# Five PSUM banks in a ring for the wide product between the two passes of layer 3

## The chip, the cores and the metric

The kernel runs on one NeuronCore of a Trainium2 chip. The metric is the device time of one execution in microseconds, lower is better. Everything happens in one launch: four layers of a graph network, each with an attention or mixing branch and a mixture-of-experts block.

## The reference, cut to what matters

There are 3125 nodes with 256 features, held as 25 tiles of 125 rows. Layer 3's graph branch is two steps of a heterogeneous graph transformer. Between the two edge passes each node row goes through this:

```python
# end of step 0, h: [3125, 256] summed messages; x: [3125, 256]
h = segment_sum(m * att[:, :, None], dst).reshape(n, 256)
h = h @ Wa[0]
x = h * sigmoid(skip[0]) + x * (1.0 - sigmoid(skip[0]))
# start of step 1: keys and values per edge type, and the query
k, q, v = x @ Wk[1], x @ Wq[1], x @ Wv[1]
kw = einsum(k[src], Watt[1][:, etype]);  m = einsum(v[src], Wmsg[1][:, etype])
```

The kernel folds `Watt` and `Wmsg` into the key and value weights beforehand. What is left for each tile is one product with a 256x256 matrix (`Wa`, the sigmoid folded in), an add, and one wide product with a 256x1280 matrix: 1024 columns go to a table in HBM from which the edges gather, and 256 are the query, which stays in SBUF. All of it is fp32.

## The kernel before, in words

The stage is one call of `renew` (name `l3_hgt0_out`, in the trace `l_hgt_out`, where digits are left out of names). `hgt` makes it with `part` (the node sums of the edge pass) and with `onward` (the wide product), and it is the only call that has both. Its engines run without a scheduler. Each has a loop over rounds `i` written out in order, and semaphores tie them. In round `i`:

- TensorE turns tile `i` of the node sums (line 1927, into `pt0`), multiplies tile `i-1` by the 256x256 matrix (line 1935, into `out0`: the first product), turns tile `i-4` of the new rows (line 1943, into `pt1`), and makes the wide product of tile `i-5` (line 1963, into `out1`). The wide product has three column groups, of 512, 512 and 256 columns, each in its own PSUM bank and with two matmuls in the code, for the two halves of the contraction. Each fp32 matmul of the code shows as two MATMULs in the trace, so a wide product is x12 there.
- VectorE divides tile `i` of the sums (line 2073), adds the first product of tile `i-1` into `x` (line 2078), and then empties two groups of the wide product of tile `i-6`: group 0, 512 columns, into `rows` (line 2118), and group 2, the query (line 2120). A drain and the signal `s_take` follow (line 2127).
- ScalarE copies the turned tiles to SBUF (lines 1976 and 1993) and empties group 1 into `rows` (line 1999, signal `s_half`).
- SyncE waits for `s_take` and `s_half` and stores the 1024 columns of the tile to the table (lines 1898 and 1899). `rows` has four slots.

PSUM has eight banks, and this stage has all of them: one for `pt0`, two for `out0`, two for `pt1`, and three for `out1`. The wide product has a single set of three banks (`B1 = 1`), so the product of tile `t` waits until both VectorE and ScalarE have emptied all of tile `t-1`:

```python
if t >= B1:
    pe.wait_ge(s_take, t - B1 + 1)
    if passing > 512 or twin:
        pe.wait_ge(s_half, t - B1 + 1)
```

Of the kernel before, what the change touches and what calls it, by code (L numbers as in the profile page):

```python
# [14 lines left out]
P = 125  # L15
# [1788 lines left out]
def renew(core, name, x, xn, mix=None, part=None, fetch=None, norm=True, onward=None, keep=None, out=None, square=None, beside=None):  # L1804
# [10 lines left out]
    passing = onward.get("passing", 0) if wide else 0  # L1815
    of, s_of = xn if norm else x, None
    mixed = part["acc"] if part else xn
    B0, B1 = (1, 1) if part and wide else (2, 2)
    last_on_vector = onward.get("last") if wide else None
    gain = fetch.get("gain") if fetch else None  # L1820
    finite = fetch.get("finite") if fetch else False
# [2 lines left out]
    with Phase(core, name) as ph:  # L1824
# [91 lines left out]
        if mix or wide:  # L1916
            @block.tensor
            def _(pe):
                for i in range(NT + 5):
                    t = i  # L1920
                    if mix and t < NT:
                        if t >= B0:
                            pe.wait_ge(s_xt0, t - B0 + 1)
                        if part:
                            pe.wait_ge(s_even, t + 1)
                        for k in range(2):
                            mm = pe.transpose(pt0[:, t % B0, P * k:P * k + P], mixed[:, t, 128 * k:128 * k + 128], core.ident[0:P, 0:P])
                        mm.then_inc(s_turn0, 1)
                    t = i - 1
                    if mix and 0 <= t < NT:  # L1930
                        pe.wait_ge(s_xt0, t + 1)
                        if t >= 2:
                            pe.wait_ge(s_x, t - 1)
                        for k in range(2):
                            mm = pe.matmul(out0[:, t % 2, 0:D], xt0[:, t % 2, k, :], a[:, k, :], start=k == 0, stop=k == 1)
                        mm.then_inc(s_mm0, 1)
                    t = i - 4
                    if wide and 0 <= t < NT:
                        pe.wait_ge(s_of, t + 1)
                        if t >= 2:  # L1940
                            pe.wait_ge(s_xt, t - 1)
                        for k in range(2):
                            mm = pe.transpose(pt1[:, t % 2, P * k:P * k + P], of[:, t, 128 * k:128 * k + 128], core.ident[0:P, 0:P])
                        mm.then_inc(s_turn, 1)
                        if square is not None:
                            for k in range(2):
                                pe.matmul(p_square[:, k, 0:D], of[:, t, 128 * k:128 * k + 128], of[:, t, :],
                                          start=t == 0, stop=t == NT - 1, skip_group_check=True)
                                mm = pe.matmul(p_square[:, k, D:D + 1], of[:, t, 128 * k:128 * k + 128], core.ones[0:P, 0:1],
                                               start=False, stop=t == NT - 1, skip_group_check=True)  # L1950
                            mm.then_inc(s_square, 1)
                    t = i - 5
                    if wide and t >= 0:
                        if t == 0 and loads:
                            pe.wait_ge(s_load, 16 * len(loads))
                        pe.wait_ge(s_xt, t + 1)
                        if t >= B1:
                            pe.wait_ge(s_take, t - B1 + 1)
                            if passing > 512 or twin:
                                pe.wait_ge(s_half, t - B1 + 1)  # L1960
                        for n, (c, d) in enumerate(cuts):
                            for k in range(2):
                                mm = pe.matmul(out1[:, t % B1, n, 0:d - c], xt_of(t)[:, k, :], w[:, k, c:d], start=k == 0, stop=k == 1)
                        mm.then_inc(s_mm, 1)

        @block.scalar
        def _(act):
            if norm:
                act.wait_ge(s_eps, 1)
            for i in range(NT + 6):  # L1970
                t = i
                if mix and t < NT:
                    act.wait_ge(s_turn0, t + 1)
                    if t >= 2:
                        act.wait_ge(s_mm0, t - 1)
                    act.copy(xt0[:, t % 2, :, :].rearrange("p k c -> p (k c)"), pt0[:, t % B0, 0:2 * P]).then_inc(s_xt0, 1)
                if gain is not None and t < NT:
                    act.wait_ge(s_var0, t + 1)
                    act.activation(sd[:, 0, t:t + 1], mv[:, 0, t, 1:2], ACT.Sqrt, bias=eps[:, 0:1]).then_inc(s_sd0, 1)
                t = i - 2  # L1980
                if norm and 0 <= t < NT:
                    act.wait_ge(s_var, t + 1)
                    act.activation(sd[:, 1, t:t + 1], mv[:, 1, t, 1:2], ACT.Sqrt, bias=eps[:, 0:1]).then_inc(s_sd, 1)
                t = i - 3
                if norm and 0 <= t < NT:
                    act.wait_ge(s_shift, t + 1)
                    act.activation(xn[:, t, :], x[:, t, :], ACT.Identity, bias=mv[:, 1, t, 0:1], scale=sd[:, 1, t:t + 1]).then_inc(s_xn, 1)
                t = i - 4
                if wide and 0 <= t < NT:
                    act.wait_ge(s_turn, t + 1)  # L1990
                    if t >= 2 and kept_xt is None:
                        act.wait_ge(s_mm, t - 1)
                    act.copy(xt_of(t).rearrange("p k c -> p (k c)"), pt1[:, t % 2, 0:2 * P]).then_inc(s_xt, 1)
                t = i - 6
                if passing > 512 and t >= 0:
                    act.wait_ge(s_mm, t + 1)
                    if t >= 4:
                        act.wait_ge(s_store[t % 4], 32 * (t // 4))
                    act.copy(rows[:, t % 4, 512:passing], out1[:, t % B1, 1, 0:passing - 512]).then_inc(s_half, 1)
                if twin and t >= 0:  # L2000
                    act.wait_ge(s_mm, t + 1)
                    act.copy(dst[:, t, 0:M - passing], out1[:, t % B1, 1, 0:M - passing]).then_inc(s_half, 1)

        @block.vector
        def _(v):
# [61 lines left out]
            for i in range(NT + 6):  # L2067
# [7 lines left out]
                if 0 <= t < NT:  # L2075
                    if part:
                        v.wait_ge(s_mm0, t + 1)
                        o = v.scalar_tensor_tensor(out=x[:, t, :], in0=part["old"][:, t, :], scalar=part["rest"], in1=out0[:, t % 2, 0:D], op0=ALU.mult, op1=ALU.add)
                        if back is not None:
                            v.wait_ge(s_back[t % 4], 32 * (t // 4 + 1))  # L2080
                            v.drain()
                            o = v.tensor_tensor(x[:, t, :], x[:, t, :], back[:, t % 4, :], ALU.add)
                        o.then_inc(s_x, 1)
                        v.drain()
                    elif mix:
                        if cvec is not None:
                            v.tensor_tensor(x[:, t, :], x[:, t, :], cvec[:, :], ALU.add)
                        v.wait_ge(s_mm0, t + 1)
                        v.drain()
                        v.tensor_tensor(x[:, t, :], x[:, t, :], out0[:, t % 2, 0:D], ALU.add).then_inc(s_x, 1)  # L2090
                        v.drain()
                    if fetch and gain is None:
                        fetched(t)
# [12 lines left out]
                                           op0=ALU.mult, op1=ALU.mult).then_inc(s_shift, 1)  # L2106
                t = i - 6
                if wide and t >= 0:
                    v.wait_ge(s_mm, t + 1)
                    if t == 0 and loads:  # L2110
                        v.wait_ge(s_load, 16 * len(loads))
                    if passing:
                        if t >= 4:
                            v.wait_ge(s_store[t % 4], 32 * (t // 4))
                        if twin:
                            v.tensor_tensor(rows[:, t % 4, :], out1[:, t % B1, 0, 0:passing], bias[:, 0:passing], ALU.add)
                        else:
                            v.tensor_copy(rows[:, t % 4, 0:min(passing, 512)], out1[:, t % B1, 0, 0:min(passing, 512)])
                    if passing and not twin:
# [1202 lines left out]
```

## Time and profile before

| | us |
|---|---|
| median of 3 runs | 7434.0 (7430.2 to 7436.23) |
| the profiled execution: its own time | 7426.5 |
| its span, first to last instruction | 7424.3 |
| this stage: first instruction of `l_hgt_out` to the last signal of its product | 5788.07 to 5992.09 |
| POOL's one wait that covers the stage and the end of the pass before | 314.4 |

The profile is one execution. Its page gives each engine's busy share of the whole span: PE (TensorE matmul) 69%, DVE (VectorE) 64%, POOL (GpSimd) 47%, ACT (ScalarE) 38%. These are averages over some forty stages with different limits, and the stage between the passes is under 3% of the span. So it has to be read from its own stretch of the timeline. In a timeline row the first number is the start in us from the start of the span, the second how long the merged instructions took, then the engine, the line of the kernel, the operation, output and inputs by name, the shape, and how many instructions were merged. In brackets stands the idle time of that engine just before, and what ended it. The end of a matmul is modelled, so the distance from one start to the next is the surer number. PEld is the load of the stationary operand, which runs beside the matmuls.

### The profile page before, as it was taken

To read this page: it belongs to the slowest core of one execution; us is meant where nothing else is said; L and a number is where in the kernel's file an instruction comes from. 1 tells how busy PE (TensorE), PEld (TensorE's weight loads), DVE (VectorE), ACT (ScalarE), POOL (GpSimd) and SP (SyncE) were. 2 spreads that over 40 slices of the span, in tenths; PEclk is the share of its full clock that TensorE was granted. 3 is DMA by queue.
4 is the path that set the end of the run, shared out by engine and by line. 5 is a ranking of instruction groups with operands and counts; after the bars stand their busy time and mean duration, and the time that the engine had idled before them with its cause. 6 is when DMAs were issued, how large, how long until landed. Compare 5 with 4: busy or idle time off the path is not lost. (4 is left out here: it accounts for less than half of the span.)

```text
span 7424.3 us, 107945 instructions
## 1 busy us (share of the span) xinstructions
PE 5125.7 (69%) x21553; PEld 3617.6 (49%) x21554; DVE 4752.9 (64%) x11861; ACT 2828.9 (38%) x6921; POOL 3525.0 (47%) x3532
## 2 busy tenths in 40 slices
PE   4763677767774967768666676877776767776764
PEld 4763444444443834558543356744444444444453
DVE  6875477677776158551556663279997369996453
ACT  2551255345534220012223222237775147772331
POOL 1776277537740257741167702236664046661014
PEclk9999877687776988979867778999998999997887
DMA  3442244324431943338334416857674156662036
GB/s 88 163 146 64 77 128 127 87 80 127 129 68 64 321 130 102 104 82 314 128 94 108 104 33 208 273 158 212 210 211 137 45 173 210 206 209 53 19 119 195
DMA packets 523813, 1021.65 MB, mean 138 GB/s; under 512 B 143645, under 2 KB 284498, under 8 KB 514846
## 3 DMA queue, kind: packets, MB, share of 16 engines
q0 software_dynamic: 191360, 489.21, 24.5%
q1 hardware_dynamic: 301663, 497.07, 20.8%
q10 hardware_dynamic: 30528, 32.52, 1.3%
q8 instruction: 87, 1.43, 0.1%
q14 instruction: 175, 1.43, 0.1%
HBM read 927.97 MB, written 90.27 MB: 137 GB/s over the span
## 5 line engine op out<-in xcount | busy, mean ns | idle before, releaser
L733 POOL DMA_INDIRECT l_hgt_ep_g<-l_tkm,l_hgt_ep_ix x832 | 922.4, 1109 | 442.8 <-PE l_hgt_ep_out L831 239.2
L744 POOL DMA_INDIRECT l_gat_ep_g<-l_gat_th,keep_e_src x832 | 865.1, 1040 | 433.8 <-issue 230.7
L831 PE MATMUL l_gat_ep_out<-l_gat_ep_g,l_gat_ep_here 128*126 128x264 f32 x1664 | 716.8, 576 | 136.6 <-DVE l_gat_acc L988 133.2
L831 PEld LDWEIGHTS l_gat_ep_out<-l_gat_ep_g,l_gat_ep_here 128*126 128x126 f32 x1664 | 394.4, 268 | 366.4 <-DVE l_gat_acc L988 297.5
L2472 DVE TENSOR_TENSOR f_moe_experts_yb<-f_moe_experts_py,f_moe_experts_b2s 128x256 f32<-128x256 f32 x208 | 88.3, 425 | 711.9 <-PE f_moe_experts_py L2455 687.5
L831 PE MATMUL l_hgt_ep_out<-l_hgt_ep_g,l_hgt_ep_here 128*126 128x288 f32 x1664 | 501.0, 425 | 55.6 <-DVE l_hgt_ep_g L974 54.0
L2423 POOL DMA_INDIRECT f_moe_experts_xg<-f_moe_tx,f_moe_tok x208 | 197.2, 948 | 699.7 <-PE f_moe_experts_px L2436 613.8
L872 ACT COPY l_gat_ep_stage<-l_gat_ep_out 30x264 f32<-30x264 f32 x832 | 307.4, 371 | 540.8 <-PE l_gat_ep_out L831 532.1
L2487 ACT ACTIVATE f_moe_experts_ht<-f_moe_experts_phid,f_moe_experts_b1b 128x128 f32<-128x128 f32 x848 | 241.3, 372 | 667.2 <-PE f_moe_experts_phid L2446 663.7
L525 POOL DMA_INDIRECT recs<-place_stage,place_pos x392 | 424.8, 1084 | 138.5 <-issue 116.8
L2744 POOL DMA_INDIRECT l_edges_g<-l_table,keep_e_src x416 | 410.3, 986 | 147.0 <-issue 120.7
L2446 PE MATMUL f_moe_experts_phid<-f_moe_experts_xt,f_moe_experts_w1b 128*128 128x128 f32 x3392 | 429.4, 281 | 68.9 <-DMA f_moe_experts_b1b<-in_L_ffn_b 60.7
L744 POOL DMA_INDIRECT l_ep_g<-l_table,keep_e_src x416 | 407.3, 979 | 126.6 <-issue 122.1
L805 PE MATMUL l_hgt_ep_found<-l_q,l_hgt_ep_hot 125*128 x1664 | 431.2, 404 | 25.5 <-ACT l_hgt_ep_hot L848 20.6
L2446 PEld LDWEIGHTS f_moe_experts_phid<-f_moe_experts_xt,f_moe_experts_w1b 128*128 128x128 f32 x3392 | 402.7, 195 | 90.6 <-issue 65.6
L831 PE MATMUL l_ep_out<-l_ep_g,l_ep_here 128*126 128x257 f32 x832 | 334.5, 556 | 106.7 <-DVE l_acc L988 100.8
L2455 PE MATMUL f_moe_experts_py<-f_moe_experts_w2b,f_moe_experts_ht 128*128 128x256 f32 x1696 | 401.4, 381 | 0.0
L872 ACT COPY l_hgt_ep_stage<-l_hgt_ep_out 126x288 f32<-126x288 f32 x832 | 307.6, 394 | 222.1 <-PE l_hgt_ep_out L831 210.0
L988 DVE TENSOR_TENSOR l_gat_acc<-l_gat_acc,l_gat_ep_out 125x264 f32 x832 | 344.3, 414 | 68.3 <-issue 48.2
L988 DVE TENSOR_TENSOR l_hgt_acc<-l_hgt_acc,l_hgt_ep_stage 125x288 f32 x832 | 370.3, 445 | 24.1 <-ACT l_hgt_ep_stage L872 14.8
L831 PEld LDWEIGHTS l_hgt_ep_out<-l_hgt_ep_g,l_hgt_ep_here 128*126 128x126 f32 x1664 | 285.7, 191 | 181.8 <-issue 133.8
L805 PEld LDWEIGHTS l_hgt_ep_found<-l_q,l_hgt_ep_hot 125*128 125x128 f32 x1664 | 310.5, 197 | 99.2 <-issue 62.0
(638 smaller groups left out, 11723.2 us busy)
## 6 DMA issues: line engine op xcount, KB each, us to landing
l_hgt_ep_hot<-locrow SPq DMA_DIRECT2D x208, 256.0 KB, 4.9
f_moe_experts_w1b<-in_L_ffn_w SPq DMA_DIRECT2D x32, 1024.0 KB, 6.5
f_moe_experts_w2b<-in_L_ffn_w SPq DMA_DIRECT2D x32, 1024.0 KB, 7.3
f_moe_experts_w1b<-in_L_ffn_w SPq DMA_DIRECT2D x64, 512.0 KB, 5.0
f_moe_experts_w2b<-in_L_ffn_w SPq DMA_DIRECT2D x64, 512.0 KB, 5.2
f_moe_experts_w1b<-in_L_ffn_W SPq DMA_DIRECT2D x56, 512.0 KB, 5.0
f_moe_experts_w2b<-in_L_ffn_W SPq DMA_DIRECT2D x56, 512.0 KB, 5.4
l_gat_ep_hot<-locrow SPq DMA_DIRECT2D x104, 256.0 KB
```

Source lines behind the costliest of these rows:

```text
L525: gp.indirect_dma_start(recs, bass.IndirectOffsetOnAxis(ap=pos[:, b, j:j + 1].bitcast(U32), axis=0), stage[:, b, j, :], None).then_inc(sca ...
L733: gp.indirect_dma_start(g[:, b % NB, j, 0:W], None, table, bass.IndirectOffsetOnAxis(ap=ix[:, b, j:j + 1].bitcast(U32), axis=0)).then_inc( ...
L744: gp.indirect_dma_start(g[:, k % NB, j, 0:W], None, table, bass.IndirectOffsetOnAxis(ap=idx[:, k * CT + j:k * CT + j + 1].bitcast(U32), ax ...
L805: mm = pe.matmul(found[:, h, j * D:j * D + D], hot[0:P, b % 2, 128 * (h * HT + j):128 * (h * HT + j) + 128], look[:, bass.ds(blks[h * HT + ...
L831: pe.matmul(out[:, t % 4, 0:WO], here[:, b % 2, t, :], g[:, b, t, F:F + WO], start=True, stop=True).then_inc(s_out, 1)
L872: act.copy(stage[lo:P + 1, b % 2, t, :], out[lo:P + 1, t % 4, 0:WO]).then_inc(s_staged, 1)
L988: v.tensor_tensor(slot, slot, stage[0:P, b % 2, t, :] if kind == "hgt" else out[0:P, t % 4, 0:WO], ALU.add).then_inc(s_added, 1)
L2423: gp.indirect_dma_start(xg[:, b, :], None, tx, bass.IndirectOffsetOnAxis(ap=tok[:, t:t + 1].bitcast(U32), axis=0)).then_inc(s_x[b], 16)
L2446: mm = pe.matmul(phid[:, b % 2, 128 * f:128 * f + 128], w1b[:, b, k, 128 * f:128 * f + 128], xt[:, b % 2, k, :], start=(k == 0), stop=(k = ...
L2455: mm = pe.matmul(py[:, b % 2, 0:D], ht[:, b % 2, f, :], w2b[:, b, f, :], start=(f == 0), stop=(f == FC - 1))
L2487: act.activation(ht[:, b % 2, f, :], phid[:, b % 2, 128 * f:128 * f + 128], func, bias=b1b[:, b, f:f + 1])
L2744: gp.indirect_dma_start(g[:, i % RB, j, :], None, table, bass.IndirectOffsetOnAxis(ap=core.e_src[:, i * EG + j:i * EG + j + 1].bitcast(U32 ...
```

## The change

Only the call with both `part` and `onward` changes (`shared` is true there). `out0` and `pt1` go from two banks to one each, and the two banks go to `out1`, which then has five. The column groups of all tiles are counted through, `3 * t + n`, and group number `g` goes to bank `g % 5`. Before TensorE writes a group it waits for the engine that empties the group five earlier, and for nothing else. For this the emptying of group 0 gets its own signal (`s_first`), next to `s_half` for group 1 and `s_take` for group 2. Group 0 and group 1 each get a signal of their own when they are made (`s_cut[0]`, `s_cut[1]`), and VectorE and ScalarE wait for these. VectorE waits for `s_mm` only before it copies group 2.

```diff
-    B0, B1 = (1, 1) if part and wide else (2, 2)
+    shared = part is not None and wide
+    B0, B1 = 1 if shared else 2, 2
...
-            out0 = ph.psum("out0", [P, 2, 512])
+            out0 = ph.psum("out0", [P, B0, 512])
...
-            pt1 = ph.psum("pt1", [128, 2, 512])
-            out1 = ph.psum("out1", [P, B1, len(cuts), 512])
+            pt1 = ph.psum("pt1", [128, B0, 512])
+            out1 = ph.psum("out1", [P, 1, 5, 512] if shared else [P, B1, len(cuts), 512])
+            s_cut = [ph.sem(f"cut{n}") for n in range(2)] if shared else []
+            s_first = ph.sem("first") if shared else None
+
+            def made_in(t, n, c):
+                return out1[:, 0, (len(cuts) * t + n) % 5, 0:c] if shared else out1[:, t % B1, n, 0:c]
...
                         pe.wait_ge(s_xt0, t + 1)
-                        if t >= 2:
-                            pe.wait_ge(s_x, t - 1)
+                        if t >= B0:
+                            pe.wait_ge(s_x, t - B0 + 1)
...
                         pe.wait_ge(s_of, t + 1)
-                        if t >= 2:
-                            pe.wait_ge(s_xt, t - 1)
+                        if t >= B0:
+                            pe.wait_ge(s_xt, t - B0 + 1)
...
                         pe.wait_ge(s_xt, t + 1)
-                        if t >= B1:
+                        if t >= B1 and not shared:
                             pe.wait_ge(s_take, t - B1 + 1)
...
                         for n, (c, d) in enumerate(cuts):
+                            if shared and len(cuts) * t + n >= 5:
+                                before, cut = divmod(len(cuts) * t + n - 5, len(cuts))
+                                pe.wait_ge((s_first, s_half, s_take)[cut], before + 1)
                             for k in range(2):
-                                mm = pe.matmul(out1[:, t % B1, n, 0:d - c], xt_of(t)[:, k, :], w[:, k, c:d], start=k == 0, stop=k == 1)
+                                mm = pe.matmul(made_in(t, n, d - c), xt_of(t)[:, k, :], w[:, k, c:d], start=k == 0, stop=k == 1)
+                            if shared and n < 2:
+                                mm.then_inc(s_cut[n], 1)
                         mm.then_inc(s_mm, 1)
...
-                    act.wait_ge(s_mm, t + 1)
+                    act.wait_ge(s_cut[1] if shared else s_mm, t + 1)
...
-                    v.wait_ge(s_mm, t + 1)
+                    v.wait_ge(s_cut[0] if shared else s_mm, t + 1)
...
+                    if shared:
+                        o.then_inc(s_first, 1)
+                        v.wait_ge(s_mm, t + 1)
+                        o = v.tensor_copy(dst[:, t, :], made_in(t, 2, M - passing))
```

No instruction changes its place on any engine. What moves are the waits. On TensorE in a round in the middle of the stage (first product, second turned tile, wide product), the order before was as follows. Semaphores are printed under the name of an earlier semaphore that had the same number: `l0_folds_cols` is `s_x`, `l0_in_store2` is `s_xt0`, `l0_in_sd` is `s_xt`, `l0_in_mm` and `l0_in_turn` are `s_half` and `s_take`.

```order
L1935 MATMUL l_hgt_out_out<-l_wa,l_hgt_out_xt 125x256 [waits l0_folds_cols,l0_in_store2]
L1935 MATMUL l_hgt_out_out<-l_wa,l_hgt_out_xt 125x256
L1943 MATMUL l_hgt_out_pt<-keep_ident,keep_x 128x125 [waits l0_in_sd,l0_folds_cols]
L1943 MATMUL l_hgt_out_pt<-keep_ident,keep_x 128x125
L1963 MATMUL l_hgt_out_out<-l_w,l_hgt_out_xt 125x512 [waits l0_in_mm,l0_in_turn,l0_in_sd]
L1963 MATMUL l_hgt_out_out<-l_w,l_hgt_out_xt 125x512 x3
L1963 MATMUL l_hgt_out_out<-l_w,l_hgt_out_xt 125x256 x2
```

In the changed kernel the same place reads as below, where `l0_mix_ms` is the new `s_first`.

```order
L1941 MATMUL l_hgt_out_out<-l_wa,l_hgt_out_xt 125x256 [waits l0_folds_cols,l0_in_store2]
L1941 MATMUL l_hgt_out_out<-l_wa,l_hgt_out_xt 125x256
L1949 MATMUL l_hgt_out_pt<-keep_ident,keep_x 128x125 [waits l0_in_sd,l0_folds_cols]
L1949 MATMUL l_hgt_out_pt<-keep_ident,keep_x 128x125
L1972 MATMUL l_hgt_out_out<-l_w,l_hgt_out_xt 125x512 [waits l0_in_mm,l0_in_sd]
L1972 MATMUL l_hgt_out_out<-l_w,l_hgt_out_xt 125x512
L1972 MATMUL l_hgt_out_out<-l_w,l_hgt_out_xt 125x512 [waits l0_in_turn]
L1972 MATMUL l_hgt_out_out<-l_w,l_hgt_out_xt 125x512
L1972 MATMUL l_hgt_out_out<-l_w,l_hgt_out_xt 125x256 [waits l0_mix_ms]
L1972 MATMUL l_hgt_out_out<-l_w,l_hgt_out_xt 125x256
```

The one wait ahead of the whole wide product for both emptying engines has become one wait ahead of each column group, each for one engine.

On VectorE a round of the same stretch was this before, where `l0_in_store3` is `s_mm0` (the first product is made), `l0_in_xn` is `s_mm` (the whole wide product is made), and `l0_in_square` is the store that last used the slot of `rows`.

```order
L2073 TENSOR_TENSOR l_hgt_acc<-l_hgt_acc,l_hgt_best 125x256
L2078 SCALAR_TENSOR_TENSOR keep_x<-keep_xn,l_alpha,l_hgt_out_out 125x256 [waits l0_in_store3]
L2118 COPY l_hgt_out_rows<-l_hgt_out_out 125x512 [waits l0_in_square,l0_in_xn]
L2120 COPY l_q<-l_hgt_out_out 125x256
L2073 TENSOR_TENSOR l_hgt_acc<-l_hgt_acc,l_hgt_best 125x256
```

It is now this, with `l0_mix_ts` for `s_cut[0]`.

```order
L2084 TENSOR_TENSOR l_hgt_acc<-l_hgt_acc,l_hgt_best 125x256
L2089 SCALAR_TENSOR_TENSOR keep_x<-keep_xn,l_alpha,l_hgt_out_out 125x256 [waits l0_in_store3]
L2129 COPY l_hgt_out_rows<-l_hgt_out_out 125x512 [waits l0_in_square,l0_mix_ts]
L2133 COPY l_q<-l_hgt_out_out 125x256 [waits l0_in_xn]
L2084 TENSOR_TENSOR l_hgt_acc<-l_hgt_acc,l_hgt_best 125x256
```

The wait for the whole product has gone from the first of the two copies to the second.

## Rows read from the trace of the kernel before

**Rows 1.** Waits from 5812 to 5996 us: in total, times, longest.

```profile
PE l_hgt_out_out L1963 <- DVEq L2127: 33.6, 21, 2.0
```

**Rows 2.** Timeline of one round in the middle: start us, us, engine, line.

```profile
5870.78 0.38 PE L1927 MATMUL l_hgt_out_pt<-keep_ident,l_hgt_acc 125*128 125x125 f32 x2
...
5871.00 1.03 PE L1935 MATMUL l_hgt_out_out<-l_wa,l_hgt_out_xt 128*125 128x256 f32 x4
...
5871.87 0.38 PE L1943 MATMUL l_hgt_out_pt<-keep_ident,keep_x 125*128 125x125 f32 x2
5872.07 0.48 DVE L2078 SCALAR_TENSOR_TENSOR keep_x<-keep_xn,l_alpha,l_hgt_out_out 125x256 f32<-125x256 f32 x1 [5.24 <-PE l_hgt_out_out L1935]
5872.28 0.37 ACT L1993 COPY l_hgt_out_xt<-l_hgt_out_pt 128x250 f32<-128x250 f32 x1 [0.71 <-PE l_hgt_out_pt L1943]
5872.55 0.59 ACT L1999 COPY l_hgt_out_rows<-l_hgt_out_out 125x512 f32<-125x512 f32 x1
5872.71 0.69 DVE L2118 COPY l_hgt_out_rows<-l_hgt_out_out 125x512 f32<-125x512 f32 x1 [0.16 <-issue]
5873.32 0.41 DVE L2120 COPY l_q<-l_hgt_out_out 125x256 f32<-125x256 f32 x1
...
5873.85 0.43 DVE L2073 TENSOR_TENSOR l_hgt_acc<-l_hgt_acc,l_hgt_best 125x256 f32<-125x256 f32 x1
5873.86 4.53 PE L1963 MATMUL l_hgt_out_out<-l_w,l_hgt_out_xt 128*125 128x512 f32 x12 [1.62 <-DVEq L2127]
...
5874.37 0.19 PEld L1963 LDWEIGHTS l_hgt_out_out<-l_w,l_hgt_out_xt 128*125 128x125 f32 x1 [0.24 <-issue]
...
5877.37 0.62 PEld L1963 LDWEIGHTS l_hgt_out_out<-l_w,l_hgt_out_xt 128*125 128x125 f32 x3 [0.24 <-issue]
...
5878.23 0.38 PE L1927 MATMUL l_hgt_out_pt<-keep_ident,l_hgt_acc 125*128 125x125 f32 x2
...
5878.45 1.03 PE L1935 MATMUL l_hgt_out_out<-l_wa,l_hgt_out_xt 128*125 128x256 f32 x4
...
5879.31 0.38 PE L1943 MATMUL l_hgt_out_pt<-keep_ident,keep_x 125*128 125x125 f32 x2
```

**Rows 3.** Timeline at the first two wide products.

```profile
5812.52 0.63 PE L1943 MATMUL l_hgt_out_pt<-keep_ident,keep_x 125*128 125x125 f32 x2
...
5812.94 6.17 PE L1963 MATMUL l_hgt_out_out<-l_w,l_hgt_out_xt 128*125 128x512 f32 x12
...
5818.94 0.38 PE L1927 MATMUL l_hgt_out_pt<-keep_ident,l_hgt_acc 125*128 125x125 f32 x2
...
5821.94 3.24 PE L1963 MATMUL l_hgt_out_out<-l_w,l_hgt_out_xt 128*125 128x512 f32 x7 [1.55 <-DVEq L2127]
```

**Rows 4.** Timeline of the last rounds, where no first product is left.

```profile
5980.72 4.53 PE L1963 MATMUL l_hgt_out_out<-l_w,l_hgt_out_xt 128*125 128x512 f32 x12 [1.04 <-ACT l_hgt_out_rows L1999]
...
5986.44 4.53 PE L1963 MATMUL l_hgt_out_out<-l_w,l_hgt_out_xt 128*125 128x512 f32 x12 [1.19 <-DVEq L2127]
...
5991.02 0.69 DVE L2118 COPY l_hgt_out_rows<-l_hgt_out_out 125x512 f32<-125x512 f32 x1 [4.70 <-PE l_hgt_out_out L1963]
5991.62 0.41 DVE L2120 COPY l_q<-l_hgt_out_out 125x256 f32<-125x256 f32 x1
5992.09 0.31 SPq L1898 DMA_DIRECT2D l_tkm<-l_hgt_out_rows  x1
```

**Rows 5.** Stretches: from:to, us, busy by engine, PE clock, DMA share, GB/s.

```profile
5760.00:5787.00 27.00, 26.44 (x97) 16.94 (x95) 19.61 (x49) 0.00 (x0) 0.00 (x0) 1.00 0.00 1
...
5870.00:5900.00 30.00, 23.16 (x81) 13.43 (x80) 7.72 (x16) 4.89 (x12) 0.00 (x0) 1.00 0.22 69
...
5963.00:5996.00 33.00, 23.31 (x66) 11.71 (x66) 5.35 (x11) 3.74 (x8) 0.31 (x2) 0.97 0.30 94
```

**Rows 6.** Timeline of the layer's earlier wide product, with two sets of banks.

```profile
4887.65 4.53 PE L1963 MATMUL f_out_out<-l_brief_w,f_out_xt 128*125 128x512 f32 x12 [0.87 <-issue]
...
4890.60 0.58 ACT L1999 COPY f_out_rows<-f_out_out 125x512 f32<-125x512 f32 x1
```

**Rows 7.** Waits of SyncE's queue from 5812 to 5996 us.

```profile
SPq L95 <- DMA l_tkm<-l_hgt_out_rows: 2.2, 1, 2.2
```

More of the change, by code:

```diff
@@ L1931, in _ @@
                         pe.wait_ge(s_xt0, t + 1)
-                        if t >= 2:
-                            pe.wait_ge(s_x, t - 1)
+                        if t >= B0:
+                            pe.wait_ge(s_x, t - B0 + 1)
                         for k in range(2):
-                            mm = pe.matmul(out0[:, t % 2, 0:D], xt0[:, t % 2, k, :], a[:, k, :], start=k == 0, stop=k == 1)
+                            mm = pe.matmul(out0[:, t % B0, 0:D], xt0[:, t % 2, k, :], a[:, k, :], start=k == 0, stop=k == 1)
                         mm.then_inc(s_mm0, 1)
@@ L1939, in _ @@
                         pe.wait_ge(s_of, t + 1)
-                        if t >= 2:
-                            pe.wait_ge(s_xt, t - 1)
+                        if t >= B0:
+                            pe.wait_ge(s_xt, t - B0 + 1)
                         for k in range(2):
-                            mm = pe.transpose(pt1[:, t % 2, P * k:P * k + P], of[:, t, 128 * k:128 * k + 128], core.ident[0:P, 0:P])
+                            mm = pe.transpose(pt1[:, t % B0, P * k:P * k + P], of[:, t, 128 * k:128 * k + 128], core.ident[0:P, 0:P])
                         mm.then_inc(s_turn, 1)
@@ L1992, in _ @@
                         act.wait_ge(s_mm, t - 1)
-                    act.copy(xt_of(t).rearrange("p k c -> p (k c)"), pt1[:, t % 2, 0:2 * P]).then_inc(s_xt, 1)
+                    act.copy(xt_of(t).rearrange("p k c -> p (k c)"), pt1[:, t % B0, 0:2 * P]).then_inc(s_xt, 1)
                 t = i - 6
                 if passing > 512 and t >= 0:
-                    act.wait_ge(s_mm, t + 1)
+                    act.wait_ge(s_cut[1] if shared else s_mm, t + 1)
                     if t >= 4:
                         act.wait_ge(s_store[t % 4], 32 * (t // 4))
-                    act.copy(rows[:, t % 4, 512:passing], out1[:, t % B1, 1, 0:passing - 512]).then_inc(s_half, 1)
+                    act.copy(rows[:, t % 4, 512:passing], made_in(t, 1, passing - 512)).then_inc(s_half, 1)
                 if twin and t >= 0:
@@ L2077, in _ @@
                         v.wait_ge(s_mm0, t + 1)
-                        o = v.scalar_tensor_tensor(out=x[:, t, :], in0=part["old"][:, t, :], scalar=part["rest"], in1=out0[:, t % 2, 0:D], op0=ALU.mult, op1=ALU.add)
+                        o = v.scalar_tensor_tensor(out=x[:, t, :], in0=part["old"][:, t, :], scalar=part["rest"], in1=out0[:, t % B0, 0:D], op0=ALU.mult, op1=ALU.add)
                         if back is not None:
@@ L2089, in _ @@
                         v.drain()
-                        v.tensor_tensor(x[:, t, :], x[:, t, :], out0[:, t % 2, 0:D], ALU.add).then_inc(s_x, 1)
+                        v.tensor_tensor(x[:, t, :], x[:, t, :], out0[:, t % B0, 0:D], ALU.add).then_inc(s_x, 1)
                         v.drain()
@@ L2117, in _ @@
                         else:
-                            v.tensor_copy(rows[:, t % 4, 0:min(passing, 512)], out1[:, t % B1, 0, 0:min(passing, 512)])
-                    if passing and not twin:
+                            o = v.tensor_copy(rows[:, t % 4, 0:min(passing, 512)], made_in(t, 0, min(passing, 512)))
+                    if shared:
+                        o.then_inc(s_first, 1)
+                        v.wait_ge(s_mm, t + 1)
+                        o = v.tensor_copy(dst[:, t, :], made_in(t, 2, M - passing))
+                    elif passing and not twin:
                         o = v.tensor_copy(dst[:, t, :], out1[:, t % B1, passing // 512, passing % 512:passing % 512 + M - passing])
```

## The prediction, made before the run

> **What bounds the kernel now.** I read the waits of the stage first, then its timeline, because the page's shares say nothing about a stage that is under 3% of the span. The list of waits has one long entry for TensorE: 21 of the 25 wide products wait for VectorE's signal behind its drain, 33.6 us in all [rows 1]. The reader is to see in one round of the timeline [rows 2] how that comes about. TensorE turns a tile at 5870.78, makes the first product at 5871.00, turns the second tile at 5871.87, and is then through at about 5872.1. But VectorE starts its add only at 5872.07, when the first product is complete. It copies group 0 at 5872.71 and the query at 5873.32, which ends at 5873.73, and only at 5873.86 does the next wide product start. The old product had been complete since before 5871. VectorE reaches it late because the add stands ahead of the copies in its order. So the stage is a loop of two engines: TensorE works 5.7 us, waits, and VectorE's chain of 2 us is exposed once per tile. The next round starts its turned tile at 5878.23, which is 7.45 us later. Nothing else is running that could hide this: DMA is busy 0.22 of the time and the clock is at its full level, 1.00 (2.4 GHz, the second row of [rows 5]). The stage ends in a barrier of all engines behind the last store [rows 7], so what it saves should come off the whole.
>
> **What a round takes without the wait.** From starts in [rows 2]: turned tile to first product 0.22 (5878.23 to 5878.45), first product to second turned tile 0.86 (to 5879.31). The second turned tile takes as long as the first, 0.22; early in the stage, where every step still took twice as long, it was 0.42 to the wide product behind it, with no wait between them (5812.52 to 5812.94) [rows 3], which fits. The wide product: weight loads at 5874.37 and 5877.37 with seven steps between them give 0.43 a step. Eight steps of 512 columns are 3.44, four of 256 columns at half that are 0.86, together 4.30. The measured 4.37 (5873.86 to 5878.23) has 0.07 more, because the first matmul behind a wait has a step of 0.50. The round is 0.22 + 0.86 + 0.22 + 4.30 = 5.60 us, against 7.45.
>
> **Do the new waits let it?** I count from the start of the second turned tile (call it 0); the wide product then starts at 0.22. Group 0 of tile t waits for ScalarE's group 1 of tile t-2, emptied a round ago. Group 1 waits for the query copy of t-2, also a round old. Group 2 waits for group 0 of t-1. VectorE adds at 0.20, copies group 0 from 0.84 to 1.53, and TensorE wants that bank at 0.22 + 3.44 = 3.66. That leaves 2.1 us. The turn of the next round needs VectorE's division (5873.85, ended 5874.28, so 2.41 on this count) at 4.52: another 2.1 us to spare. VectorE has 0.48 + 0.69 + 0.41 + 0.43 = 2.0 us of work in the round and ScalarE 0.37 + 0.37 + 0.59 = 1.3, so TensorE is the bound by far.
>
> **The banks given up.** With one bank for the first product, the product of tile t has to wait for the add of t-1. VectorE does this add before it divides tile t+1, and TensorE has already waited for that division in order to turn tile t+1. So the new wait is always met: cost nothing, and it can't cost anything. With one bank for the second turned tile, the next turn waits for ScalarE's copy, which ends 0.78 after the turn started (5871.87 to 5872.65) [rows 2], while the next turn comes 5.6 us later, or 4.5 in the last rounds. Nothing either.
>
> **The extra waits and signals.** Each wide product has three waits for banks, two of them in its middle, where before there was none. No row shows a met wait inside a wide product. The nearest rows are the joints between the turned tiles and the first product, which carry waits too and follow each other in 0.22 and 0.86 us, exactly what the matmuls take: 0. From the other side, a wait that really stops TensorE costs, beyond its length, 0.13 from the end of the query copy to the start (5873.73 to 5873.86) and the 0.07 of the slow first step, 0.20; three in each of 24 products would be 14.4 us. Below nothing is excluded, since a wait takes no matmul away. I take 0, because the joints are the same case: waits that are met before TensorE gets there. The wait added on VectorE and the two signals lie inside its 3.6 us of idle time per round.
>
> **The copies beside matmuls.** VectorE and ScalarE now read PSUM while TensorE writes other banks. In the earlier stage of the same form ScalarE's copy took 0.58 in the middle of a wide product [rows 6], against 0.59 here beside an idle TensorE [rows 2]. Cost 0.
>
> **The sum.** Tiles t = 0 to 24, from the start of wide product 0. To the next turned tile 6.00 (5812.94 to 5818.94, its first steps still twice as long) [rows 3], as before; then 1.30 to wide product 1. From 1 to 19, 18 rounds of 5.60 = 100.8. From 19 to 20 no tile of the sums is left to turn: 4.30 + 0.86 + 0.22 = 5.38. From 20 to 23 only the second turn is left: 3 x 4.52 = 13.56. From 23 to 24: 4.30. Together 131.3. Before, it was 5986.44 - 5812.94 = 173.5 [rows 3, 4]. Saved: 42.2. At the end the 512-column copy no longer waits for the whole product, so the query copy follows it at once: 5991.62 - 5991.02 = 0.6 [rows 4]. In all 42.8 us. A check from the other side: 33.6 us of waits [rows 1], and about 1.04 each for the three that ended on ScalarE (one is the first row of [rows 4]), are 36.7; the rows start an idle time at the modelled end of a matmul, some 0.16 late, and each restart costs 0.07, so 24 x 0.23 = 5.5 more: 42.2.
>
> The profiled execution took 7426.5, of which 7424.3 is its span; its sum is 7426.5 - 42.8 = 7383.7. The median of the runs is 7.5 above the profiled one, and I carry the saving over to it: 7434.0 - 42.8 = 7391.2.
>
> **Stores.** A tile's 500 KB now leaves every 5.6 us, and every 4.5 in the last rounds, 111 GB/s. At one tile per 5.75 us the queues moved 94 GB/s at a share of 0.30 (the third row of [rows 5]), so 0.36 is asked for. The last store landed within 2.2 us of its issue [rows 7], and four slots give 18 us. Nothing.
>
> **Rivals.**
>
> A, the waits inside the product show (8%): between the bounds above, up to 14.4 us of the gain is lost. At two thirds, 9.6, the time is 7401. Against it stand the joints in [rows 2].
>
> B, a new wait takes the place of the old one (4%): TensorE stands before group 2 until VectorE has emptied group 0. It decides once VectorE is 2.1 us later than in my count, for instance if its copies slowed beside matmuls. If only the query copy and its drain were hidden (0.5 a round, 24 times), the gain would be 12 us: 7422. Against it: ScalarE's copy in [rows 6].
>
> C, no effect (3%): the ring still waits for the same signal, or the next pass starts earlier and gives it back in its gathers: 7434. Against it: group 1's wait is for a tile older, as the changed order shows, and the barrier lies between.
>
> D, slower (3%): TensorE's clock falls in the stage. At 1.2 GHz a round would be 11.2 us, 3.75 more than now. For 18 rounds that is 67 us, and 9.0 against 5.75 in the last five another 16: some 7517. It decides from the point at which a third of a round is at the half clock (5.60 x 1.33 = 7.45). Against it: with TensorE busy 26.44 of 27.00 us the clock was 1.00, and at 23.16 of 30.00, with an idle gap in each round, also 1.00 [rows 5]; the ring makes those gaps smaller.
> The Trainium skill has a rule for this (TensorE: Matmul & The Clock Gate, "A second HAM failure mode: psum-queue depth-cycling"): a kernel that cycled through PSUM banks each iteration left small idle gaps between groups of matmuls, and its clock swung between the two levels. By that rule rival D would hold, by the two rows of 1.00 it doesn't; the trace so far disagrees with it.
>
> **How the numbers follow.** My forecast, all waits gone, has 82%: 7391. Its own range comes from the differences between runs (the profiled one 7.5 below the median, the three 6 apart) and from half of the bound on waits. For 8 in 10 I take 7382 to 7404; the upper end holds nearly all of rival A. Faster than 0.2% means below 7419; 0.2% is about what a measurement of this kernel can tell from no change. Forecast and A are faster, B is about half on either side: faster 0.93, same 0.04, slower 0.03.
>
> **What would show it.** In the new profile the distance between wide products in the middle is 5.6 us, with no idle time of PE before or inside a wide product; the row "PE waits for DVEq" of this stage is gone or under 1 us; VectorE's add follows each first product as before, and its wait there shrinks from 5.24 to about 3.4; the group 0 copy of the last tile starts before the product is complete; the whole stage is some 43 us shorter, and all stages behind it take as long as before. I am wrong if PE idles in steps of 0.2 inside a product (A), if it waits before group 2 (B), or if the clock is under 1.00 between the first and last wide product (D).

## The result

The changed kernel took 7391.1 us in the median of 5 runs (7383.2 to 7398.6), the kernel before, measured again beside it, 7430.2 (7417.4 to 7436.2). The ratio is 0.9949 with a 95% interval of 0.9937 to 0.9960: 38 us, or 30 to 47. A second set of runs on another chip gave 0.9937 (0.9920 to 0.9953). The prediction was 7391.2 and a gain of 42.8 us.

The span of the new profiled execution is 7383.8 us, 40.5 less. The first view is again one round in the middle of the stage, now of the changed kernel, with the columns of [rows 2].

```profile
5870.24 0.38 PE L1933 MATMUL l_hgt_out_pt<-keep_ident,l_hgt_acc 125*128 125x125 f32 x2
...
5870.46 1.03 PE L1941 MATMUL l_hgt_out_out<-l_wa,l_hgt_out_xt 128*125 128x256 f32 x4
...
5871.32 0.38 PE L1949 MATMUL l_hgt_out_pt<-keep_ident,keep_x 125*128 125x125 f32 x2
...
5871.53 0.48 DVE L2089 SCALAR_TENSOR_TENSOR keep_x<-keep_xn,l_alpha,l_hgt_out_out 125x256 f32<-125x256 f32 x1 [3.39 <-PE l_hgt_out_out L1941]
5871.54 4.46 PE L1972 MATMUL l_hgt_out_out<-l_w,l_hgt_out_xt 128*125 128x512 f32 x12
...
5872.17 0.69 DVE L2129 COPY l_hgt_out_rows<-l_hgt_out_out 125x512 f32<-125x512 f32 x1 [0.16 <-issue]
...
5872.77 0.41 DVE L2133 COPY l_q<-l_hgt_out_out 125x256 f32<-125x256 f32 x1
...
5873.31 0.43 DVE L2084 TENSOR_TENSOR l_hgt_acc<-l_hgt_acc,l_hgt_best 125x256 f32<-125x256 f32 x1
...
5875.84 0.38 PE L1933 MATMUL l_hgt_out_pt<-keep_ident,l_hgt_acc 125*128 125x125 f32 x2
```

The wide product starts 0.22 after the second turn with no bracket of idle time, where it had waited 1.62 us in [rows 2]. VectorE does the same things at the same distance from the first product as before, but nobody waits for them. From turn to turn it is 5.60 us (5870.24 to 5875.84) against 7.45.

The next rows are the last tile, and the stretch from product 1 to near the end of product 24, in the order of engines of [rows 5].

```profile
5940.82 8.76 PE L1972 MATMUL l_hgt_out_out<-l_w,l_hgt_out_xt 128*125 128x512 f32 x24
...
5947.04 0.69 DVE L2129 COPY l_hgt_out_rows<-l_hgt_out_out 125x512 f32<-125x512 f32 x1 [1.29 <-PE l_hgt_out_out L1972]
...
5949.62 0.42 DVE L2133 COPY l_q<-l_hgt_out_out 125x256 f32<-125x256 f32 x1 [1.89 <-PE l_hgt_out_out L1972]
5950.10 0.31 SPq L1904 DMA_DIRECT2D l_tkm<-l_hgt_out_rows  x1
```

```profile
5821.00:5949.00 128.00, 128.00 (x446) 74.90 (x445) 42.88 (x87) 27.22 (x66) 0.00 (x0) 1.00 0.31 97
```

TensorE is busy for all 128 us. From 5812 us on, where the list of [rows 1] began, it has one wait left, in the head and for VectorE's division. The second row is POOL's one wait that covers the stage, 314.4 us before:

```profile
PE l_hgt_out_pt L1933 <- DVE l_hgt_acc L2084: 0.8, 1, 0.8
POOL l_hgt_ep_ix L725 <- POOLq L95: 269.6, 1, 269.6
```

The row of 33.6 us [rows 1] is gone. The waits ahead of 5812 us, five for the division and 12.8 us in all, are in both kernels. I measure the stage from its first VectorE instruction (line 2006 before, 2017 after) to the issue of the last tile's first store. Before, that was 5788.07 to 5992.09, 204.0 us. Now it is 5789.64 to 5950.10, 160.5 us.

### The profile page after: what moved, and what is told of

It reads as the page before. It is cut to its first block and busy times, and to the rows that moved or that the text cites. A ratio compares the mean times of both kernels' runs of the same rounds, so it can differ in the third digit from the quotient of the medians.

```text
span 7383.8 us, 107946 instructions
## 1 busy us (share of the span) xinstructions
PE 5110.4 (69%) x21553; PEld 3608.4 (49%) x21554; DVE 4756.1 (64%) x11861; ACT 2831.3 (38%) x6921; POOL 3529.4 (48%) x3532
## 5 line engine op out<-in xcount | busy, mean ns | idle before, releaser
L805 PE MATMUL l_hgt_ep_found<-l_q,l_hgt_ep_hot 125*128 x1664 | 432.9, 405 | 26.7 <-ACT l_hgt_ep_hot L848 21.7
```

The source lines that it names most:

```text
L805: mm = pe.matmul(found[:, h, j * D:j * D + D], hot[0:P, b % 2, 128 * (h * HT + j):128 * (h * HT + j) + 128], look[:, bass.ds(blks[h * HT + ...
```

## The experiments

All stage lengths below are taken from the traces in that way. Rounds are the distances between the starts of successive wide products. A median is to be compared only with the one beside it, which was taken on the same chip, since chips differ.

| kernel | stage us | middle round | last rounds | median | before beside it | ratio (95%) |
|---|---|---|---|---|---|---|
| before | 204.0 | 7.45 | 5.79 | | | |
| changed | 160.5 | 5.60 | 4.51 | 7391.1 | 7430.2 | 0.9949 (0.9937 to 0.9960) |
| e1_ring3 | 190.4 | 7.13 | 4.51 | 7408.2 | 7418.3 | 0.9987 (0.9978 to 0.9996) |
| e2_order | 192.1 | 6.86 | 5.78 | 7407.9 | 7418.3 | 0.9983 (0.9974 to 0.9992) |
| e3_order_ring3 | 160.9 | 5.60 | 4.51 | 7380.2 | 7418.3 | 0.9950 (0.9937 to 0.9963) |
| e5_late_signals | 161.6 | 5.60 | 4.51 | 7379.1 | 7418.3 | 0.9944 (0.9930 to 0.9959) |
| a0_changed_again | 160.7 | 5.60 | 4.51 | 7385.4 | 7428.7 | 0.9937 (0.9920 to 0.9953) |
| e4_ring4 | 161.1 | 5.60 | 4.51 | 7382.6 | 7428.7 | 0.9936 (0.9919 to 0.9953) |
| e6_waits | 160.7 | 5.60 | 4.51 | 7387.9 | 7428.7 | 0.9945 (0.9928 to 0.9962) |
| e7_slow5 | 182.4 | 6.65 | 4.51 | 7403.0 | 7428.7 | 0.9959 (0.9945 to 0.9973) |
| e10_order_both | 169.1 | 5.72 | 5.72 | 7978.9 | 8011.0 | 0.9949 (0.9930 to 0.9968) |
| e8_ring4_slow2 | 178.3 | 6.55 | 4.51 | 7992.7 | 8011.0 | 0.9970 (0.9950 to 0.9989) |
| e9_front | 147.4 | 5.60 | 4.51 | 7950.2 | 8011.0 | 0.9915 (0.9894 to 0.9936) |
| e11_front_again | 147.3 | 5.60 | 4.51 | 7358.1 | 7423.4 | 0.9910 (0.9897 to 0.9924) |

### Signals and split waits without more banks (e1_ring3)

Against the changed kernel, cut:

```diff
-            out1 = ph.psum("out1", [P, 1, 5, 512] if shared else ...)
+            out1 = ph.psum("out1", [P, 1, 3, 512] if shared else ...)
...
-                            if shared and len(cuts) * t + n >= 5:
+                            if shared and len(cuts) * t + n >= 3:
```

`out0` and `pt1` have two banks again, and group `g` goes to bank `g % 3`.

> The new signals and one wait per column group, but in the old three banks (first product and second turned tile keep their two). Theory (TensorE stood because VectorE emptied the single set of banks late, behind its add): group 0 of a tile now waits only for the copy of group 0 of the tile before, which ends 0.7 to 0.8 us before the drain behind the query copy did less the 0.13 restart; a round in the middle goes from 7.45 to 7.1, the last rounds from 5.75 to 4.5; together 13 us less than before, 7417 by the first median. Rival (the signals and the split wait are what paid, not the two banks): most of the 40 us, about 7392. Rival (nothing without banks): 7430.

Measured: rounds of 7.13, last rounds 4.51, the stage 13.6 us shorter, the whole 0.9987. The signals alone carry the last rounds and a third of a microsecond per middle round, as the theory said. One round of e1 (the stretch shown ends inside the wide product, so its row has fewer than x12; so it is in the rows of e2 and e8):

```profile
5885.92 0.38 PE L1949 MATMUL l_hgt_out_pt<-keep_ident,keep_x 125*128 125x125 f32 x2
5886.13 0.48 DVE L2089 SCALAR_TENSOR_TENSOR keep_x<-keep_xn,l_alpha,l_hgt_out_out 125x256 f32<-125x256 f32 x1 [4.93 <-PE l_hgt_out_out L1941]
...
5886.77 0.69 DVE L2129 COPY l_hgt_out_rows<-l_hgt_out_out 125x512 f32<-125x512 f32 x1 [0.16 <-issue]
...
5887.60 1.95 PE L1972 MATMUL l_hgt_out_out<-l_w,l_hgt_out_xt 128*125 128x512 f32 x4 [1.30 <-DVE l_hgt_out_rows L2129]
```

The product starts 0.14 after the copy of group 0 ends, and that copy still stands behind the add.

### Another order instead of more banks (e2_order, e10_order_both)

e2 is the kernel before with VectorE's copies moved ahead of its add. `emptied` holds the two copies, the drain and the signal, unchanged.

```diff
                     v.tensor_tensor(m3, m3, ...).then_inc(s_even, 1)
+                if part and wide:
+                    emptied(i - 6)
                 t = i - 1
```

> The kernel before with one edit: VectorE empties the wide product ahead of its add instead of behind it. Banks and waits are the old ones. Theory (what put the emptying late was its place behind the add): the two copies now run beside the turned tile and the first product, the wide product starts 1.35 to 1.45 us after the round's first turn instead of 3.15, a round takes 5.72 to 5.79, the last rounds stay at 5.75; 33 to 35 us less than before, 7396. Rival (only more banks can free TensorE): 0 to 10 us less, 7425. Rival (the add is now late and holds TensorE): slower than before by up to 0.5 a round, 7440.

Measured: rounds of 6.86, not 5.75; the stage 12.0 us shorter, the whole 0.9983. My sum was wrong, and the timeline of e2 says where:

```profile
5886.35 0.69 DVE L2079 COPY l_hgt_out_rows<-l_hgt_out_out 125x512 f32<-125x512 f32 x1 [4.73 <-PE l_hgt_out_out L1963]
...
5886.96 0.41 DVE L2081 COPY l_q<-l_hgt_out_out 125x256 f32<-125x256 f32 x1
...
5887.65 0.37 ACT L1993 COPY l_hgt_out_xt<-l_hgt_out_pt 128x250 f32<-128x250 f32 x1 [0.71 <-PE l_hgt_out_pt L1943]
5887.91 0.59 ACT L1999 COPY l_hgt_out_rows<-l_hgt_out_out 125x512 f32<-125x512 f32 x1
...
5888.65 0.67 PE L1963 MATMUL l_hgt_out_out<-l_w,l_hgt_out_xt 128*125 128x512 f32 x1 [1.04 <-ACT l_hgt_out_rows L1999]
```

VectorE is through at 5887.37, as expected, but ScalarE empties group 1 only at 5887.91, because in its order this copy stands behind the copy of the second turned tile. Before, ScalarE finished 0.6 us ahead of VectorE's second copy [rows 2], so the list of waits named only VectorE. It was the last of two, and the other was almost as late. e10 moves ScalarE's copy (`second`) to the head of its round too.

```diff
             for i in range(NT + 6):
+                if part and wide:
+                    second(i - 6)
                 t = i
                 if mix and t < NT:
                     act.wait_ge(s_turn0, t + 1)
```

> The kernel before, with the old banks and waits, but VectorE and ScalarE both empty the wide product first in their round. In the run with VectorE alone, the wide product started 1.04 us after TensorE was free, behind ScalarE's copy of group 1, which stands behind two copies of turned tiles. Theory (any engine that empties late holds the single set of banks; the order is the cause, more banks are one cure): rounds of 5.7 to 5.8, last rounds as before at 5.75, 32 to 35 us less than the kernel before and 7 to 9 us more than the changed kernel. Rival (something else holds TensorE at 6.86): no gain over that run, 12 us less than before in the stage.

Measured: rounds of 5.72 throughout, the stage 34.9 us shorter than before and 8.6 longer than in the changed kernel, the whole 0.9949. Two code blocks in another place, with no new bank and no new signal, give four fifths of what the stage gained. In e10's timeline the wide product starts 0.26 after the second turn, and the row names VectorE's drain only four times in the stage:

```profile
PE l_hgt_out_out L1963 <- DVEq L2095: 4.1, 4, 1.2
```

### Order and signals, three banks (e3_order_ring3)

This is e1 with VectorE's copies first.

> Both: VectorE empties first, and the three old banks have one wait and one signal each. Theory: group 0 is emptied 1.0 us after the round's first turn and wanted at 1.30, groups 1 and 2 later still, so no wait is left anywhere: rounds of 5.60, last rounds 4.52, the same time as the changed kernel (40 to 43 us less than before, 7390) with two banks to spare. Rival (five banks are needed): 5 or more us slower than the changed kernel.

Measured: rounds of 5.60, the stage 160.9 us, the whole 0.9950. It equals the changed kernel with three banks in the ring. Five banks are sufficient, but not necessary. In this run the two others are back with `out0` and `pt1`, so all eight are in use; a ring of three with one bank each for `out0` and `pt1`, which would leave two free, was not run.

### How many banks, and how much slack (e4_ring4, e7_slow5, e8_ring4_slow2)

e4 is the changed kernel with four banks in the ring and two for the first product. e7 has five more copies on VectorE ahead of the copy of group 0, into a tile nobody reads:

```diff
+                            for j in range(5 if shared else 0):
+                                v.tensor_copy(spare[:, j, :], made_in(t, 0, 512))
                             o = v.tensor_copy(rows[:, t % 4, 0:min(passing, 512)], made_in(t, 0, min(passing, 512)))
```

e8 is e4 with two such copies.

> The changed kernel again, as the measure for the three runs beside it. Theory: 40 to 43 us less than the kernel before on the same chip, stage of 160.5 us from its first instruction to the last store.

> Four banks in the ring, the first product keeps two. Theory: group 1 now waits for the copy of group 0 of the tile before, ready 1.66 us after the second turn and wanted at 1.94: no wait, the same time as with five banks. Rival (the fifth bank is needed): 0.2 to 1 us more in each of 20 rounds, 4 to 20 us slower than the changed kernel.

> The changed kernel with five more 512-column copies on VectorE ahead of each copy of group 0 (0.61 us from start to start, 3.05 a round). Theory (2.1 us to spare in front of group 2's bank and of the next division): the round becomes 6.7 to 6.8 instead of 5.60, 21 to 24 us slower than the changed kernel; VectorE has then 5.0 us of work in a round, so it is the late signal and not VectorE's load that binds. Rival (no slack, every added us shows): 20 x 3.05 = 61 us slower. Rival (VectorE's lateness no longer matters with five banks): 0.

> Four banks in the ring and two more 512-column copies on VectorE ahead of the copy of group 0 (1.22 us a round). Theory (with four banks the slack is 0.3 us, with five 2.1): group 1 waits 0.9 to 1.0 us, rounds of 6.5 to 6.6, 17 to 20 us slower than the changed kernel. Rival (four banks are as good as five in every respect): no wait, as the changed kernel.

Measured: a0 160.7 us, with no wait for a bank. e4 161.1 us; in 17 of its 18 middle rounds no matmul is held up (5.59 or 5.60 each). Of the 0.4 us more, 0.3 lie in the first wide product and 0.13 in one round of 5.72. There VectorE came to the copy of group 0 0.37 late, and the weight load for group 1 had to wait for it:

```profile
5879.92 0.69 DVE L2129 COPY l_hgt_out_rows<-l_hgt_out_out 125x512 f32<-125x512 f32 x1 [0.53 <-issue]
...
5880.66 0.29 PEld L1972 LDWEIGHTS l_hgt_out_out<-l_w,l_hgt_out_xt 128*125 128x125 f32 x2 [0.69 <-DVE l_hgt_out_rows L2129]
```

In the changed kernel one copy starts just as late (at 5878.13, idle 0.53 before it), and no round is longer for it. e7 182.4 us, 21.7 more, with rounds of 6.65; e8 178.3 us, 17.6 more than a0, with rounds of 6.55. In the stage e7 and e8 lie in their ranges, and a0 and e4 within 0.7 us of the changed kernel's 160.5; of the whole e7 lost 18 us in the medians. e8 ran on another chip than a0, so only its stage is compared. A round of e7:

```profile
5879.78 3.08 DVE L2132 COPY l_hgt_out_spare<-l_hgt_out_out 125x512 f32<-125x512 f32 x5 [0.16 <-issue]
5882.78 0.68 DVE L2133 COPY l_hgt_out_rows<-l_hgt_out_out 125x512 f32<-125x512 f32 x1
...
5883.52 1.13 PE L1974 MATMUL l_hgt_out_out<-l_w,l_hgt_out_xt 128*125 128x256 f32 x4 [0.77 <-DVE l_hgt_out_rows L2133]
```

TensorE has made groups 0 and 1 and stands before group 2, the place that the prediction's rival B named. The five copies put the copy of group 0 off by 3.00 us (5879.78 to 5882.78) and cost 1.05 a round, so 2.0 were slack; I had counted 2.1. With four banks the stop comes before group 1. The rows of e8:

```profile
6445.73 0.68 DVE L2133 COPY l_hgt_out_rows<-l_hgt_out_out 125x512 f32<-125x512 f32 x1
...
6446.47 1.98 PE L1974 MATMUL l_hgt_out_out<-l_w,l_hgt_out_xt 128*125 128x512 f32 x4 [0.69 <-DVE l_hgt_out_rows L2133]
```

There 1.2 us of work cost 0.95, so the slack is 0.3. The fifth bank buys 1.7 us of slack, of which this kernel would have used 0.1, in one round.

### The signals for finished groups, and what a met wait costs (e5_late_signals, e6_waits)

```diff
-                    act.wait_ge(s_cut[1] if shared else s_mm, t + 1)
+                    act.wait_ge(s_mm, t + 1)
...
-                    v.wait_ge(s_cut[0] if shared else s_mm, t + 1)
+                    v.wait_ge(s_mm, t + 1)
```

> The changed kernel, but VectorE and ScalarE wait for the whole wide product before their first copy, as before (the two signals for finished groups are not used). Theory: in the rounds both engines reach these waits a round late anyway, so only the end of the last tile loses, 0.6 us: the stage as in the changed kernel within 1 us, 7391. Rival (the early signals carry the last rounds): rounds of 4.5 go back to 5.75, 6 us slower than the changed kernel.

Measured: 161.6 us with the same rounds. That is 1.2 us more than the changed kernel, a little over the 1 us expected, and 0.9 more than a0. Of the 1.2, 0.6 are at the end, from the start of the last product to the last store 5.58 instead of 4.98, as expected. The other 0.6 lie in the first round, 7.28 against 6.69. The granted clock rises from 0.50 to 1.00 inside that product, and not at the same place in every run: in a0, the same code as the changed kernel, the round took 6.94.

e6 doubles the waits inside the product. ScalarE gives the three signals `s_more` behind each copy of a second turned tile:

```diff
                             for k in range(2):
+                                if shared and k == 1 and t >= 2:
+                                    pe.wait_ge(s_more[n], t - 1)
                                 mm = pe.matmul(made_in(t, n, d - c), ...)
```

> The changed kernel with three more waits in each wide product, one before the second matmul of each group, on signals that ScalarE gave a tile ago; so six waits instead of three, all met. Theory: a met wait costs TensorE nothing here, stage as in the changed kernel within 1 us. Rival A of the prediction (waits show, up to 0.20 each): up to 0.20 x 3 x 23 = 14 us slower than the changed kernel.

Measured: 160.7 us, the same as a0 to the tenth, rounds of 5.60. Rival A's price of up to 0.20 for each wait is excluded: three more in each of 23 tiles cost nothing in the stage, from product 0 to product 24 130.9 us as in a0.

### A better head (e9_front, e11_front_again)

In the changed kernel TensorE is the bound from product 1 on, so what is left of this stage is its head: 24.85 us to the first wide product, 6.2 of them VectorE's maximum and reciprocal over all tiles. e9 takes them by tile, and divides one tile further ahead.

```diff
-                v.tensor_scalar(part["den"], ones_of, part["least"], None, ALU.max)
...
-                v.reciprocal(part["den"], part["den"])
...
+            if part and wide:
+                divided(0)
+                divided(1)
             for i in range(NT + 6):
...
+                if part and wide and t >= 1:
+                    divided(t + 1)
```

`divided(t)` is the maximum, the reciprocal and the product for one tile.

> The changed kernel with another head of the stage: VectorE no longer takes the reciprocal of all 25 tiles at once (6.2 us in which TensorE stands) but tile by tile, and divides one tile further ahead. Theory: the first turn starts 5.5 us earlier, the five first rounds take 2.7 instead of 3.54 us each, and the middle stays at 5.60 since VectorE has 3.4 us to spare: 8 to 10 us less than the changed kernel, 50 us less than before. Rival (TensorE's low clock in the head eats it, or the added small instructions bind): 0 to 4 us less than the changed kernel.

> The version with the new head once more, since its first run was on a chip on which all kernels take 8% longer. There the stage took 147.4 us from its first instruction to the last store, against 160.5 to 161.7 in the changed kernel. Theory: the stage takes 147 to 148 us wherever it runs, and on a chip on which the kernel before takes 7420 to 7430 the total is 57 us less than before, 7365 to 7375, 13 less than the changed kernel. Rival (the other stages give part of it back): 40 to 45 us less than before, as the changed kernel.

Measured: 147.4 and 147.3 us, 13.1 to 13.4 less than the changed kernel's stage, rounds of 5.60 as before. The stage gave more than the 8 to 10 us expected of it. The whole is 0.9910 (0.9897 to 0.9924) of the kernel before, 65 us in the medians, of which the stage accounts for 56.7; 57 were expected, and 7358.1 lies below the range of 7365 to 7375. Where the rest comes from was not looked into. It has the shortest stage and the lowest ratio. As a whole time it is not shown to be the fastest: its interval lies below the changed kernel's in the first comparison (0.9937 to 0.9960) but touches the one in the second (0.9920 to 0.9953), and the two were never on one chip together. Rows of e11's head:

```profile
5797.53 0.35 DVE L2087 RECIPROCAL l_hgt_best<-l_hgt_best 125x32 f32<-125x32 f32 x1
...
5798.45 0.68 PE L1933 MATMUL l_hgt_out_pt<-keep_ident,l_hgt_acc 125*128 125x125 f32 x2 [2.89 <-DVE l_hgt_acc L2090]
...
5802.64 1.86 PE L1941 MATMUL l_hgt_out_out<-l_wa,l_hgt_out_xt 128*125 128x256 f32 x4 [0.25 <-DVE keep_x L2107]
...
5805.16 1.10 PE L1941 MATMUL l_hgt_out_out<-l_wa,l_hgt_out_xt 128*125 128x256 f32 x4 [0.45 <-ACT l_hgt_out_xt L1987]
...
5809.85 1.45 PE L1972 MATMUL l_hgt_out_out<-l_w,l_hgt_out_xt 128*125 128x512 f32 x3
```

The head takes 12.75 us, 12.1 less. Another 1.1 come from the first wide product: the distance to the next one is 5.60 us instead of 6.69, since all of it is at the full clock. My sum had left out TensorE's clock. The product with the 256x256 matrix takes 1.86 at 5802.64 and 1.10 at 5805.16: the clock rises between them. The granted clock of the two heads, the changed kernel's first:

```profile
5789.60:5814.50 24.90, 13.13 (x37) 8.74 (x38) 10.76 (x14) 2.57 (x7) 0.00 (x0) 0.56 0.00 1
```

```profile
5797.10:5809.80 12.70, 9.77 (x36) 6.73 (x37) 8.51 (x26) 2.50 (x7) 0.00 (x0) 0.73 0.00 0
```

0.56 is nearly all at the low level, 1.2 GHz. In the new head TensorE is busy 77% of the time instead of 53%, and the mean is 0.73.

## Why the prediction was right

- **What bounds.** TensorE waited for the emptying of a single set of banks. Shown: the wait is gone with five banks, with four but for one round, and with three, a signal for each and another order; and e7 brings a wait back at the place that was named. What the prediction said too narrowly is that VectorE was the cause. e2 shows that ScalarE's order alone costs 1.1 us a round (6.86 against 5.72 in e10). For the forecast it made no difference, since the ring frees TensorE of both.
- **A round of 5.60.** Measured 5.59 or 5.60 in all 18 middle rounds. VectorE's wait before its add shrank from 5.24 to 3.39, for the 3.4 named, and its copies take beside the matmuls what they took before (0.69 and 0.41). The last rounds 4.51 for 4.52, the last product's step 4.30 for 4.30. The stores ask for 0.38 of the DMA there (5931.8 to 5945.1 us) for 0.36, and hold nothing up.
- **The sum.** From product 0 to product 24: 130.6 us for 131.3, the difference in the first product, which caught more of the full clock (5.39 us for 6.00; in a0, 130.9). The end: 0.67 for 0.6.
- **The banks given up cost nothing.** In the changed kernel TensorE has no wait for `s_x` or `s_xt` in the stage. e4, which gives one of them back, is the same.
- **Waits and signals cost nothing.** I had taken the lower bound of 0 to 14.4 us. The rounds of 5.60 and e6 show it.
- **The whole.** The stage lost 43.6 us, the span of the profiled execution 40.5. The rest is the other stages: this one began 1.6 us later than in the kernel before, and the part behind it took 1.5 more. In the runs on chips of like speed, with the same code ahead of the stage, it began anywhere from 5782 to 5801. So the total of one execution can't confirm the sum to better than some 10 us. The stage can, and the medians (38 and 47 us by the two ratios) lie on both sides of 42.8.
- **The clock.** It stayed at 1.00 from product 1 to the end, at 128.00 us busy of 128. In the kernel before it was 1.00 too where TensorE was busy 77% of the time [rows 5], with a gap of 1.6 us in each round. The Trainium skill (TensorE: Matmul & The Clock Gate, "A second HAM failure mode: psum-queue depth-cycling") describes a bf16 kernel that cycles through PSUM banks and whose small idle gaps between groups of matmuls let its clock swing. The two traces here, both fp32, show no swing: the ring cycles and leaves no gap, and the kernel before left gaps.
- **Luck.** 7391.1 against 7391.2 is closer than the method deserves. The kernel before moved from 7434.0 to 7430.2 in its own median when measured again, so the gain in the medians was 39.1 for the 42.8 forecast, and the two differences cancel.
- **A slip.** The chances of the forecast, of rival A and of half of rival B add up to 0.92, not to the 0.93 that is stated for faster. Nothing else hangs on it.

## What to carry to other kernels

Where an engine waits for the emptying of a PSUM buffer, look at what stands ahead of the copies in every engine that empties it, since the list of waits names only the last: moving the copies to the head of the round on both engines gave 35 of 44 us here without a new bank, and moving VectorE's alone, with a signal for each of the three banks, gave 43. Compute the slack of each new wait from one round of the timeline, which was right to 0.1 us here. When a loop has reached its bound, look at its head: here TensorE waited there and also ran at its low clock.

## What was not expected of the hardware

- The head of the stage, 12.1 us shorter for an expected 8 to 10: TensorE's first instruction there comes 1.35 us after the stage's start instead of 6.96 and its waits are shorter, and the granted clock was at 0.50 for 6.8 us instead of 23.9 (27.3 in the kernel before). How much of the 12.1 the clock gave, and whether the denser start is what raised it sooner, no run tried by itself.
- On one chip every kernel took 8% longer (8011 us for the kernel before, against 7418 to 7430), while this stage took the same there to 0.1 us (147.4 and 147.3 in the two runs of the same kernel). The mean granted clock over the whole was 0.83 there (0.825 to 0.833) and 0.85 to 0.86 elsewhere. What made the other stages longer was not looked into.
